# A small U-shaped convolution network on one core: all of level 0 moved to plain fp32 in 64x64 tiles, image after image

## The reference, cut to what matters

```python
x  = gn(x)                                   # mean and variance of each image and channel
x  = basic_block(x, e0b0c1, e0b0c2)          # level 0, 64x64
x  = basic_block(x, e0b1c1, e0b1c2); f0 = x
x  = basic_block(x, e1b0c1, e1b0c2, stride=2, ds=e1b0ds)   # level 1, 32x32
x  = basic_block(x, e1b1c1, e1b1c2); f1 = x
x  = basic_block(x, e2b0c1, e2b0c2, stride=2, ds=e2b0ds)   # level 2, 16x16
x  = basic_block(x, e2b1c1, e2b1c2)
x  = (relu(deconv2(x, dec0w) * S) + f1) * S
x  = (relu(deconv2(x, dec1w) * S) + f0) * S
# basic_block: relu(conv3(relu(conv3(x, w1)), w2) + identity), each conv 3x3 with 32 channels in and out
```

## Time and profile before

| what | value |
|---|---|
| median of 3 runs | 86.38 us (86.05, 86.38, 87.48) |
| the profiled execution, whole time | 87.17 us |
| its span, first to last instruction | 85.4 us |
| outside the span | 1.77 us |
| PE, PEld, DVE, ACT, POOL busy | 78.6, 65.9, 52.7, 45.3, 17.6 us |
| granted TensorE clock, mean | 0.996 |

### The profile page before, as it was taken

The page is one execution under the profiler, slowest core; times in us unless marked ns, Lnnn a source line. Parts: engine busy times, 40 slices in busy tenths (PEclk is TensorE's granted clock), DMA queues, the critical chain, the costliest instruction groups (busy, mean ns, idle before and its releaser), DMA issues.

```text
span 85.4 us, 2024 instructions
## 1 busy us (share of the span) xinstructions
PE 78.6 (92%) x775; PEld 65.9 (77%) x775; DVE 52.7 (62%) x172; ACT 45.3 (53%) x102; POOL 17.6 (21%) x38
## 2 busy tenths in 40 slices
PE   4989999999999999999999999999999999799800
PEld 3757999998677877777687777999999999587500
DVE  5569969889605777052333657999797977212640
ACT  6005504992105329999252149799999997000400
POOL 7400042610000000005792000100288200000230
PEclk9999999999999999999999999999999999999998
DMA  1867950032581605740000000000000000000084
GB/s 20 247 167 242 367 218 0 0 90 78 183 217 65 154 0 144 228 113 22 0 4 0 0 0 0 0 0 0 8 0 0 0 4 0 0 8 0 0 299 193
DMA packets 4185, 6.55 MB, mean 77 GB/s; under 512 B 464, under 2 KB 2128, under 8 KB 4176
## 3 DMA queue, kind: packets, MB, share of 16 engines
q1 hardware_dynamic: 4032, 6.29, 23.8%
q10 hardware_dynamic: 144, 0.13, 0.5%
HBM read 5.37 MB, written 1.05 MB: 75 GB/s over the span
## 4 chain that ended last, share of the span: by engine, by line
PE 86%; DVE 4%; DMA 4%; issue 1%; DVEq 0%
PE psum L927 53%; PE psum L1026 25%; PE psum L979 4%; DMA x_sb<-x_in 4%; DVE late_b L916 2%; DVE stats L699 2%; PE psum L1212 1%; PE psum L995 1%; PE psum L967 1%; PE psum L1259 1%; PE psum L988 1%; DVEq L195 0%; DVE last L841 0%; DVE flat L839 0%; PE psum L972 0%
## 5 line engine op out<-in xcount | busy, mean ns | idle before, releaser
L927 PE MATMUL psum<-shared,w_e0b0c 128*128 128x364 f32 (+2 forms) x72 | 12.5, 333 | 0.0
L927 PEld LDWEIGHTS psum<-shared,w_e0b0c 128*128 128x128 f32 x72 | 12.0, 195 | 0.1
L1026 PE MATMUL psum<-late_b,w_e0b1c 64*64 64x264 f32 (+2 forms) x192 | 11.0, 384 | 0.0
L1026 PE MATMUL psum<-late_a,w_e0b0c 64*64 64x256 f32 (+2 forms) x96 | 10.6, 376 | 0.0
L1026 PE MATMUL psum<-late_a,turned_e0b0c 64*64 64x256 f32 (+2 forms) x96 | 10.6, 376 | 0.0
L1026 PEld LDWEIGHTS psum<-late_b,w_e0b1c 64*64 64x64 f32 x192 | 8.0, 132 | 2.7
L537 POOL TENSOR_TENSOR odd<-relu,odd 128x264 fp32r<-128x264 f32 (+1 forms) x8 | 5.2, 681 | 22.7 <-ACT odd L629 22.6
L979 PE MATMUL psum<-zeros 128*128 128x256 bf16 x37 | 8.2, 399 | 1.1 <-DVE eps L752 1.1
L1026 PEld LDWEIGHTS psum<-late_a,w_e0b0c 64*64 64x64 f32 x96 | 6.7, 132 | 2.0 <-issue 0.2
L860 DVE SCALAR_TENSOR_TENSOR relu<-psum,inside 128x290 f32<-128x290 f32 (+2 forms) x8 | 3.6, 446 | 6.3 <-PE psum L1026 6.0
L1026 PEld LDWEIGHTS psum<-late_a,turned_e0b0c 64*64 64x64 f32 x96 | 6.7, 132 | 0.9
(11 more groups left out here) (143 smaller groups left out, 143.4 us busy)
## 6 DMA issues: line engine op xcount, KB each, us to landing
x_sb<-x_in SPq DMA_DIRECT2D x4, 160.0 KB, 3.1
raw<-e0b0c_in SPq DMA_DIRECT2D x2, 256.0 KB, 3.6
raw<-e0b1c_in SPq DMA_DIRECT2D x2, 256.0 KB, 4.1
raw<-e1b1c_in SPq DMA_DIRECT2D x2, 256.0 KB, 2.6
raw<-e2b1c_in SPq DMA_DIRECT2D x2, 256.0 KB, 2.7
raw<-e1b0c_in SPq DMA_DIRECT2D x1, 448.0 KB, 4.2
raw<-e2b0c_in SPq DMA_DIRECT2D x1, 448.0 KB, 4.0
x_sb<-x_in SPq DMA_DIRECT2D x2, 192.0 KB, 3.2
```

Source lines behind the costliest of these rows:

```text
L927: last = pe.matmul(within(target, columns), w, within(moving, columns), start=(first and n == 0), stop=(final and n == len(terms) - 1), sk ...
L1026: last = pe.matmul(target, weights_of, moving, start=first, stop=final, skip_group_check=True)
```

## The change: what it does

All four stages of level 0 become tiled fp32 stages. The two pieces that share the array are now rows of the upper half and rows of the lower half (from `TURNED_FROM` = 16 on, with swapped halves) of one image, and the images are done one after the other: a group of four pieces (`GROUP`) is one image of one stage. Odd stages have 34 rows in their pieces where there were 33 (row 16 is computed in both halves).

The split of the normalised map and of the weights of e0b0c1 and e0b1c2 goes away; e0b0c1's weights are loaded straight into place. e0b1c2 gets turned weights. The map is normalised into `flat_plain` by DVE (rows 0 to 22) and by ACT in two steps (rows 23 to 31). The high planes of e0b1c2 are still made by ACT piece by piece, with the four pieces of an image; the low planes by DVE once for an image (`low_planes`). Sides, corners and `scale_skip0` of image 0 now stand on ACT together, behind the last piece of image 0.

```diff
-NORM_ROWS = [(0, 12), (12, 20)]
-LOW_ROWS = [(12, 11), (23, 9)]
+NORM_BY_DVE = [(0, 9), (9, 14)]
+NORM_BY_ACT = (23, 9)
-TILED = {"e0b0c2": [[(0, 9), (9, 8)], [(17, 8), (25, 7)]], "e0b1c1": [[(0, 9), (9, 8)], [(17, 8), (25, 8)]]}
+TILES = {"odd": [(0, 9), (24, 9), (9, 8), (16, 8)], "even": [(0, 8), (24, 8), (8, 8), (16, 8)]}
+TURNED_FROM = BLOCKS[0] // 2
+GROUP = 4
...
-            for row, rows in sum(TILED[stage.name], []):
-                for i in range(IMAGES):
+            for i in range(IMAGES):
+                for row, rows in TILES[stage.kind]:
                     pieces.append(Piece(s, len(pieces), range(i, i + 1), row, rows))
...
             for piece in LEVEL0:
-                if STAGES[piece.stage].name == "e0b0c1":
+                stage = STAGES[piece.stage]
+                if stage.name == "e0b0c1":
                     weights_hi(piece.index + 1)
+                if stage.kind == "odd":
                     continue
                 wait_relu(act, piece.index)
...
+                for i in range(2):
+                    last = act.activation(planes1_inside(0, piece.images[0], i, piece.row // 2, piece.rows // 2),
+                                          fp32_of(piece)[:, i::2].rearrange("p r (c b) -> p b r c", b=2), ACT.Relu)
+                last.then_inc(hi_ready, 1)
+                if piece is LEVEL0[-GROUP - 1]:
                     gather_sides(1, 0)
-                if piece is LEVEL0[-2]:
-                    gather_corners(1, 0, range(2))
...
+                    gather_corners(1, 0)
+                    scale_skip0(0)
+            gather_sides(1, 1)
             gather_corners(1, 1)
             scale_skip0(1)
...
+            def low_planes(image):
+                for i, j in [(0, 0), (0, 1), (1, 0), (1, 1)]:
+                    lo, hi = [plane1_inside(half, image, i, j) for half in (1, 0)]
+                    last = dve.scalar_tensor_tensor(out=lo, in0=block0[:, image, i::2, j::2], scalar=0.0,
+                                                    in1=hi.bitcast(F32), op0=ALU.max, op1=ALU.subtract)
+                last.then_inc(lo_kept, GROUP)
...
+                dve.tensor_scalar(s[:, 6:7], mean, -1.0, None, ALU.mult).then_inc(mean_negated, 1)
...
+                for row, rows in NORM_BY_DVE:
+                    dve.tensor_scalar(flat_inside(image, row, rows), x_sb[:, image, row:row + rows, :], mean,
+                                      s[:, 5:6], ALU.subtract, ALU.mult).then_inc(norm_by_dve, 1)
...
+                if stage.name == "e0b1c2" and piece.index == source_of_level(1, image):
                     wait_half(dve, piece.index, 0)
-                    for i, j in [(0, 0), (0, 1), (1, 0), (1, 1)]:
...
+                    low_planes(image)
+                if piece.index in (source_of_level(level, image) for level in (1, 2)):
                     wait_half(dve, piece.index, 1)
                     first = SIDES_BY_ACT[stage.level + 1, image]
                     side_copies(stage.level + 1, image, first, len(SIDES) - first)
...
-                    h = c if main == (image == 0) else 1 - c
...
+                    h = c if main != flipped else 1 - c
+                    o = 1 - c if stage.kind == "odd" and flipped else c
+                    w = turned[stage.name] if stage.kind == "even" and flipped else w_sb[W_INDEX[stage.name]][:, 0]
...
+                        if pieces[0].index == 0 and m == 1 and n == 1:
+                            sum_stats(1)
...
+            for first in range(0, len(LEVEL0), GROUP):
+                tile_group(STAGES[LEVEL0[first].stage], LEVEL0[first:first + GROUP])
```

More of the change, by code:

```diff
@@ L121 @@
 STAGES = [
[L122 to L125, removed]
+    Stage("e0b0c1", "odd", 0, 9),
+    Stage("e0b0c2", "even", 0, 8, residual="flat"),
+    Stage("e0b1c1", "odd", 0, 9),
+    Stage("e0b1c2", "even", 0, 8, residual="block0"),
     Stage("e1b0c1", "down", 1, 17),
@@ L363, in made_by @@
             stage = STAGES[piece.stage]
-            if stage.name == "e0b0c1":
+            if stage.tiled and stage.kind == "odd":
                 return relu_ready
@@ L416, in fp32_of @@
         def fp32_of(piece):
-            if STAGES[piece.stage].name == "e0b0c1":
-                return odd_plain[:, piece.images[0], piece.row:piece.row + piece.rows, :]
+            if STAGES[piece.stage].tiled and STAGES[piece.stage].kind == "odd":
+                return odd_plain[:, piece.images[0], slot_of(piece):slot_of(piece) + piece.rows, :]
             if STAGES[piece.stage].residual is not None:
                 return block0[:, piece.images[0], piece.row:piece.row + piece.rows, :]
-            return relu_of(piece) if STAGES[piece.stage].level else rows_0(relu_of(piece), piece)
+            return relu_of(piece)
         def split_of(piece, half):
[L426 to L431, removed]
+            return odd1[:, half, piece.images[0]]
         def dec0_sums(row, j):
@@ L524, in _ @@
             ground(flat2[:], 2)
[L526 to L538, removed]
-            pool.wait_ge(summed, last_piece(STAGE["e0b1c2"], range(IMAGES), BLOCKS[0] - 1) + 1)
-            ground(flat1.bitcast(F32).rearrange("p h i n -> p (h i) n"), 1)
-            wait_half(pool, last_piece(STAGE["e1b0c1"], range(IMAGES), 0), 1)
+            ground(flat1[:].bitcast(F32).rearrange("p h i n -> p (h i) n"), 1)
             for image in range(IMAGES):
                 pool.wait_ge(skip0_scaled, image + 1)
+                if image == 1:
+                    wait_half(pool, last_piece(STAGE["e1b0c1"], range(IMAGES), 0), 1)
                 pool.tensor_tensor(normed[:, image], normed[:, image], x_sb[:, image], ALU.add).then_inc(skip0_added, 1)
@@ L812, in _ @@
                 sums = sums_of(piece)
-                if stage.residual is None and not stage.from_bank and stage.name != "e0b0c1":
+                if stage.kind == "odd" and stage.level == 1:
                     before = PIECES[piece.index - RELU_SLOTS]
@@ L861, in _ @@
                                                         op0=ALU.max, op1=ALU.mult)
-                    elif stage.residual == "normed":
-                        dve.wait_ge(norm_ready, 2 * image + 2)
-                        last = dve.tensor_tensor(target, normed[:, image, rows, :], sums, ALU.add)
+                    elif stage.residual == "flat":
+                        dve.wait_ge(norm_by_dve, len(NORM_BY_DVE) * (image + 1))
+                        dve.wait_ge(norm_by_act, image + 1)
+                        last = dve.tensor_tensor(target, flat_inside(image, piece.row, piece.rows), sums, ALU.add)
                     else:
@@ L1051, in mains_before @@
             def mains_before(pieces):
-                return sum(STAGES[p.stage].tiled for p in PIECES[:pieces[0].index]) // 2
+                return pieces[0].index // 2
             pe.wait_ge(ground_set, 1)
@@ L1083, in _ @@
                 target = sums_of(piece)
-                flat_columns = piece.rows * FLAT_PITCH + piece.rows * FLAT_PITCH % 2
-                if stage.kind == "odd" and level == 0:
-                    target = bank_of(piece)[:, 0:flat_columns]
-                elif level == 0:
-                    target = rows_0(target, piece)
                 terms = []
@@ L1113, in moving @@
                         return split0[:, half, images[0], sy % 2, sx % 2, first:first + RUN[1]]
-                    if stage.kind == "odd" and level == 0:
-                        first = (piece.row + sy) * FLAT_PITCH + sx
-                        return flat0[:, half, images[0], first:first + flat_columns]
-                    if level == 0:
-                        return odd[0][:, half, images[0], piece.row + sy:piece.row + sy + piece.rows,
-                                      sx:sx + BLOCKS[0]]
                     source, run = (odd1, EVEN_RUN[1]) if stage.kind == "even" else (flat1, RUN[1])
```

323 lines of the change are left out of this document (103 added, 220 removed).

## The result

| | before | after |
|---|---|---|
| median | 86.35 us (4 runs, 86.05 to 87.48) | 90.88 us (4 runs, 90.67 to 91.36) |
| ratio to before, 95% interval | | 1.054 (1.048 to 1.060) |
| profiled execution, its span | 87.17, 85.4 us | 90.79, 88.6 us |
| outside the span | 1.8 us | 2.2 us |

The change makes the kernel 4.5 us slower where 2.5 was forecast. In a second comparison the same two kernels gave 90.12 against 86.17, ratio 1.042 (1.034 to 1.051). Ratios are taken over the undisturbed executions alone.

The account below looks back on a forecast made before the run. PE bounds the kernel. Level 0 gives -1.25 us and waits at the hand-over to level 1 +3.7, so +2.5 on a median of 86.38: 88.9 us, range 87.9 to 90.2, at 55%.

Parts of the forecast that it names:

- Level 0 on PE: Level 0's four stages on PE: 11.9, 10.4, 11.3 and 10.4 us, together 1.25 us less (0.8 to 1.7).
- The hand-over: Image 1's results into e1b0c1 of level 1: PE waits 1.9, 0.5 and 1.2 us, +3.7 from waits.
- +2.5: End of e1b0c1 of image 1 moves by +2.5 us: -1.25 from level 0, +3.7 from waits.
- Cover 0.3: Start of e0b0c1: image 0's normalised map ready near 8.5, PE arrives at 8.8 behind its warm-up.
- T: Time when PE is through with level 0: 52.9 us, where it was 54.13.
- Behind it nothing is late next: After e1b0c1 of image 1: no further waits on DVE, corners or sides; every later step moves by 2.5 us.
- Span 85.4 + 2.5: Final sum: span 87.9, 89.7 profiled with 1.77 outside; that one lay 0.8 above the median, so 86.38 + 2.5 = 88.9.
- (1): Rival: hand-over to level 1 stays hidden, only level 0's gain shows; 85.1, more honestly 85.9 us; 12%.
- (2): Rival: hand-over waits partly shorter, 2.2 us instead of 3.7, DVE not held by POOL; +1.0, 87.4 us; 15%.
- (3): Rival: PE's clock falls in the hand-over pauses, next products take twice as long; +1.7 to 2.0, 90.8 us; 10%.
- (4): Rival: a level 0 stall put down as covered (image 1's normalisation or e0b0c2's results) opens; +0.5 to 1, 89.7; 8%.
- POOL locks DVE's combined form: DVE's low planes of image 1: POOL's addition may hold up multiply-subtract; no row shows it; without it 0.35 lower.

Follow-up runs that it names:

- experiment 1: Changed kernel with ACT's four corners and scaling of image 0 moved behind the planes and sides of image 1: 87.42 us, ratio to before 1.019.
- experiment 7: Changed kernel with image 0's corners spread over ACT's idle gaps around the planes and sides of image 1: 86.35 us, ratio to before 1.005.
- experiment 4: Kernel before with ACT's sides, four corners and scaling of image 0 in one block behind image 0's last piece: 90.88 us, ratio 1.059.
- experiment 2: Changed kernel with POOL's first addition waiting for e1b0c1, as before the change: 89.59 us, ratio to before 1.034.
- experiment 5: Changed kernel unedited, run again for the spread and a second trace: 90.12 us, spans from 87.2 to 89.2.
- experiment 3: Changed kernel with 15 and 8 filler products on PE in the waits for image 1's high planes and sides: 89.45 us.
- experiment 8: Kernel before with each of its 32 first warm-up products cut in eight of 32 columns: 86.90 us, span 85.0.
- experiment 10: Changed kernel with the memory of the result and of the scaled skip exchanged: 89.5 us, span 87.3.

## Why the prediction was right in its mechanism and wrong in its size

**Level 0 on PE** was right: four stages within 0.15 us each, no wait of PE in it, 1.0 us gained at its end (forecast 1.25).

**The hand-over** was right in its place, its order and its waits. The forecast was 1.9, 0.5 and 1.2 us on ACT's planes, DVE's low planes and DVE's side copies. The early trace of the changed kernel has just these three:

```profile
56.76 1.52 PE L843 MATMUL psum<-split,w_e1b0c 128*128 128x290 f32 x10 [1.91 <-ACT split L595]
58.67 0.91 PE L843 MATMUL psum<-split,w_e1b0c 128*128 128x274 f32 x5 [0.38 <-DVE split L726]
60.65 2.57 PE L843 MATMUL psum<-shared,w_e1b0c 128*128 128x290 f32 x18 [1.07 <-DVE shared L718]
63.06 0.54 PE L843 MATMUL psum<-shared,w_e1b0ds 128*128 128x272 f32 x3
```

Experiments 1 and 7 show the first cause, ACT's block, by taking it away, experiment 4 by putting it into the kernel before.

**What was mis-sized** can be read from two traces with the same, early start (span 84.1 before, 87.3 after). These are the marks of PE in each:

| mark | before | after | difference |
|---|---|---|---|
| first product of e0b0c1 | 7.90 | 8.54 | +0.64 |
| first product of e1b0c1 | 52.90 | 51.86 | -1.04 |
| shortcut products of e1b0c2, image 0 | 60.02 | 63.06 | +3.04 |
| first product of level 2 | 68.76 | 72.04 | +3.28 |
| span | 84.1 | 87.3 | +3.2 |
| whole time | 85.97 | 89.51 | +3.54 |

The two traces with the late start (spans 85.4 and 88.6) give nearly the same differences: +0.42, -1.01, +3.07, +3.30, +3.2 and +3.62.

Against the +2.5 of the prediction, four terms are off.

(a) **"Cover 0.3" at the start was no cover.** It was computed behind a warm-up at 1.2 GHz, which only the executions with the late start have. In the others PE is free at 7.6 and the start is the normalisation's: DVE's two blocks take 0.99 us where the one block took 0.48, and the first product comes 0.64 later. In the late traces it comes 0.42 later (8.82, now 9.24), with no idle time shown: it stands 3.1 us behind the start of the 14 warm-up products in all five late traces with the new arithmetic, and 2.8 in both with the old. It is now the first product in 64x64 tiles after 128x128 ones; no run isolates whether that is the reason. The saving of level 0's products (45.0 to 43.3 from start to end) hid all this in the end mark, which is why T was nearly right: 0.2 of the miss.

(b) **The waits.** The sum put 3.75 us for the hand-over (from -1.25 to +2.5); the marks give 3.04 + 1.04 = 4.08, 0.3 more. Counted from the end of level 0, the high planes came within 0.1 us of the forecast. The low planes took 2.07 us beside POOL where 1.8 were put, and the side products started after 8.8 us where 8.5 were put.

The three idle times add to 3.36 only, 0.7 less than the 4.08. The rows show why. PE in the trace of the kernel before with the early start:

```profile
55.77 2.07 PE L927 MATMUL psum<-split,w_e1b0c 128*128 128x290 f32 x15
57.69 2.50 PE L927 MATMUL psum<-shared,w_e1b0c 128*128 128x290 f32 x18
60.02 0.53 PE L927 MATMUL psum<-shared,w_e1b0ds 128*128 128x272 f32 x3
```

Here image 1's 15 products take 1.92 us from the first to the next group, 0.128 each. In the changed kernel they stand as ten and five, busy for 1.52 and 0.91 us, where 0.128 each gives 1.28 and 0.64. The last product before a pause is counted for its whole length, 0.29 us, where in an unbroken run its successor starts 0.13 us after it. That and the slower first step behind a pause is 0.5 of the 0.7.

(c) **"Behind it nothing is late next" failed:** POOL's second addition meets the identity addition, +0.24 from the third mark to the fourth; experiment 2, where that addition takes 1.34 us for 2.08, does not have it. I had moved all of that by 2.5 and not looked at who meets whom after the shift.

(d) **Outside the span** +0.34, taken as constant; the cause stays open.

Together 0.2, 0.3, 0.24 and 0.34, less 0.1 given back behind the fourth mark, lead from +2.5 to +3.5.

**The rest, from +3.5 to the +4.5 of the first comparison,** is the mixture of executions. The changed kernel had the late start in all four of its first runs, by their spans of 88.5 to 89.1, and before in the profiled one but not in its median. Of the ten executions of the changed kernel three had the early start. Whether the change makes the late start more frequent isn't settled: experiments 1, 3 and 7, with the same start, have it in 7 of 20 executions. As far as the runs show, four late starts out of four were chance; the six executions of experiment 5 had three, and a median of 90.12.

**The step that failed** is the last of the sum: "Span 85.4 + 2.5" carried over to a median by a constant offset, when the profiled execution lay 0.8 above its median because of its start. Of the 2.0 us between 88.9 and 90.88 this step made 1.0, and the four terms above the other half.

The rivals: (1) and (2) fell. (3) came true in part: the clock fell to half behind the pause in the profiled execution and cost nothing there, and in experiment 2 it cost at most 0.3 us, not 1.7 to 2.0. Two executions of the changed kernel with a mean clock of 0.962 took some 0.6 us longer than the other late ones; none such was traced, so where the clock fell in them is not known. (4) fell: neither of its two places shows a wait. The stall that did open is that of image 0's start, in (a). That POOL locks DVE's combined form, left open in the prediction, is shown by experiment 2.

## What to carry to other kernels

A strict queue is a place in time for every instruction in it. When work for the next piece is put in one block, ask what the block's last instruction delays, and put what is wanted late into the gaps of what is wanted early: here moving five instructions on ACT was worth 3.4 us (experiment 7 against the changed kernel, early starts), the new arithmetic of four stages 1. If a profiled execution lies apart from its median, compare executions of the same kind, and find out what it has of its own before using it as the base of a sum: a cover that exists only in it is no cover. After each shift in a sum, go once more through the pairs of engines that hold each other up.

## What the runs showed of the hardware that was not expected

- The moment when TensorE's clock rises differed between executions of one kernel: 14 products of 256 columns took 3.17 us in some and 1.70 in others, and the whole time moved by 1.1 to 1.3 us with it.
- The clock fell to 0.50 behind a pause of 1.92 us in the changed kernel's first trace and behind one of 1.90 in experiment 2. It stayed at 1.00 through a pause of 1.91 us in experiment 5 and through one of 3.29 in experiment 4. The length of the pause alone did not decide it.
- A pause of PE costs more than the idle time shown for it: 0.24 and 0.27 us more for two of them in experiment 5, by the spacing of the products.
- The first 15 products of 128x128 after a stretch in 64x64 tiles are busy for 2.18 to 2.20 us, where the same 15 after 128x128 products take 2.07. But from the first of them to the group behind it is 2.01 to 2.04 us against 1.99, so hardly any of this is lost.
- DVE's combined multiply-subtract with two SBUF operands waits for a running POOL addition just as a plain addition does (2.08 us for four instead of 1.43; for plain additions 2.01 and 2.08 instead of 0.46 and 0.44).
- Programs of the changed kernel have 2.1 to 2.2 us outside the span, those of the kernel before 1.8 to 1.9, and neither 448 more instructions on PE (experiment 8) nor other buffers of the stores (experiment 10) moved that.
